# Last attention layer: the zero test of the score sums, one turn of the loop later

## The chip, the cores and the metric

The kernel runs on one core of a Trainium2 chip. The metric is the device time of one execution in microseconds (us); the median of several runs counts. The engines are called by the profile's names: PE (matrix products), DVE (vector), ACT (activations), POOL (GpSimd), SP (issues the DMAs).

## The reference

Four layers run over 64 graphs of 128 nodes with 384 features: an attention over a masked adjacency, two kinds of directed graph convolution (the second kind twice), and a last attention. Ahead of each layer stands a layer norm with ReLU, and its result is added to x. Only the last layer is touched. Per graph it is, cut to what matters (12 heads of 32 features, k = 128 keys):

```
h = maximum(layernorm(x), 0)
q, k, v = heads of h @ Wq.T, h @ Wk.T, h @ Wv.T + bv
a = einsum('bnhd,bmhd->bhnm', q, k) * SCALE + encoding_bias[:, None]
pad_mask = all(a == 0, axis=-1)
a = where(pad_mask[..., None], -inf, a)
a = nan_to_num(softmax(a, axis=-1))
o = einsum('bhnm,bmhd->bnhd', a, v)
x = x + o @ Wo.T + bo
```

A row of scores that is zero throughout gives a row of zeros in a. The kernel does this by a factor per row and head, called keep: 1 if the row's minus-maximum or the sum of its scores is not zero, else 0.

## The kernel before, in words

Each engine has a program of its own for a layer; semaphores tie them. In an attention layer every engine's program is one function, step, that is run for the turns t = 0, 1, 2, ... and writes the order of that engine's work out by hand. A turn works on several graphs at once: a helper called as f(n_, k) works on graph t + k, and n_.has(k) says whether that graph exists. Turns 0 to 3 and the last ones are unrolled, those between are a loop whose body holds two turns. In a turn, graph t gets its scores, t + 1 its projections q and k, t + 2 its norm, t − 1 its probabilities and their product with v, t − 2 its scaling, output projection and result. Tiles that live over a turn have two slots, by t mod 2 (keep and the minus-maxima are among them; the score sums, nonzero, rsum and rnorm have one).

**PE**, in a turn: the scores (L834), then it waits for attended of t − 2 and turns it (L859), projects q and k of t + 1 (lines 149 to 151, weights by hT), projects the output of t − 2 (lines 149 to 151, w by oT), turns the probabilities of t − 1 (L841), projects v (lines 149 to 151), turns h of t + 2 (L804) and multiplies probabilities by v (L850 to L852). Each product is three, as both sides are split into a high and a low half-precision part.

**DVE**, in a turn: row_sums (the reciprocal of the sums that PE's product gave, L697), drop_masked (in the last layer only a wait for the adjacency tile), row_scales (rnorm = rsum × scale × keep, L704), score_bias (L644), attend (attended = product × rnorm, L713), stats (L621), the first four heads of biased_max (scores and their maxima, L665), mean_var, o_split (L718), four heads, var_eps (L630, L631), four heads; score_sums of t − 1 (L673), nonzero_sums (L677), kept_rows (L681), add_result of t − 2 (L725), three p_split (L692), v_split (v_lo, L686), turned_lo (hT_lo, L652).

**POOL**, in a turn: add_out_bias (L499), norm (L483, L485), fold_scores (L505, then L509: the 128 scores of each row and head are added to 64 and to 32 sums; score_sums adds those to one). It waits for all maxima of the turn before it folds.

**ACT**, in a turn: exponentials (L550), o_split (L577), q_evict (L557), normed (L537), k_evict (L562), three p_split (L572), v_split (v_hi, L567), turned_hi (L543).

A helper waits by `wait(dve, semaphore, value)`, an instruction of its own, also for results of its own engine. In the loop the value is a register worked out from the loop's index the first time that a turn of the body needs it. ssum and nonzero are written and read by DVE alone, and in the engine's order; the next writer of ssum waits only for POOL.

```
def nonzero_sums(n_, k):
    wait(dve, ssum_ready, n_.done(k, base=0))
    dve.tensor_scalar(nonzero[:, :], ssum[:, :], 0.0, None, ALU.not_equal).then_inc(nonzero_ready, 1)

def kept_rows(n_, k):
    wait(dve, nonzero_ready, n_.done(k, base=0))
    dve.scalar_tensor_tensor(out=keep[:, n_.slot(k), :], in0=nmax[:, n_.slot(k), :], scalar=0.0,
                             in1=nonzero[:, :], op0=ALU.not_equal, op1=ALU.max).then_inc(keep_ready, 1)
```

Of the kernel before, what the change touches and what calls it, by code (L numbers as in the profile page):

```python
# [139 lines left out]
def wait(eng, sem, value):  # L140

    if isinstance(value, int) and value <= 0:
        return
    eng.wait_ge(sem, value)
# [9 lines left out]
def build(nc, ins, out):  # L154
    with ExitStack() as ctx:
        def sb(stack, name, shape, dt=F32):
            return stack.enter_context(nc.sbuf_tensor(name, shape, dt))
# [189 lines left out]
        def attention(tag, weights, last_layer, next_weights, extras, bias_rows=None, v_bias=None, minus_beta=None, out_bias=None):  # L347
# [7 lines left out]
            with ExitStack() as s:  # L355
# [72 lines left out]
                with nc.Block() as block:  # L428
# [186 lines left out]
                    def _(dve):  # L615
                        dve.wait_ge(tables_ready, 1)

                        def stats(n_, k):
                            if not last_layer:
                                wait_apart(dve, (x_loaded, n_.done(k, 16)))  # L620
                            dve.bn_stats(bn[:, :], x[:, n_.graph(k), :]).then_inc(stats_done, 1)  # L621

                        def mean_var(n_, k):
                            wait_apart(dve, (stats_done, n_.done(k)))
                            dve.bn_aggr(mv[:, :], bn[:, :]).then_inc(mean_ready, 1)

                        def var_eps(n_, k):
                            wait(dve, ln_ready, n_.done(k - 1))
                            wait(dve, mean_ready, n_.done(k))
                            dve.tensor_scalar(ve[:, 0:1], mv[:, 1:2], EPS_PRE, None, ALU.add)  # L630
                            dve.tensor_scalar(ve[:, 1:2], mv[:, 0:1], -1.0, None, ALU.mult).then_inc(var_ready, 1)  # L631

                        def drop_masked(n_, k):
                            wait(dve, adj_loaded, n_.done(k, 16))
                            if not last_layer:
                                wait(dve, bias_ready, n_.done(k - 1))
                                dve.tensor_scalar(drop[:, :], adj_tile[:, n_.slot(k), :], 0.0, -MASKED, ALU.is_le,
                                                  ALU.mult).then_inc(drop_ready, 1)

                        def score_bias(n_, k):  # L640

                            a = adj_tile[:, n_.slot(k), :]
                            if last_layer:
                                dve.tensor_scalar(bias[:, n_.slot(k), :], a, -1.0, None, ALU.mult).then_inc(bias_ready, 1)  # L644
                            else:
                                wait(dve, drop_ready, n_.done(k))
                                dve.scalar_tensor_tensor(out=bias[:, n_.slot(k), :], in0=a, scalar=minus_beta[:, 0:1],
                                                         in1=drop[:, :], op0=ALU.mult, op1=ALU.add).then_inc(bias_ready, 1)

                        def turned_lo(n_, k):  # L650
                            wait(dve, hT_hi, n_.done(k))
                            dve.tensor_tensor(hT[1][:, n_.slot(k), :], hT_bank[:, 0:D], hT[0][:, n_.slot(k), :],  # L652
                                              ALU.subtract).then_inc(hT_lo, 1)
# [21 lines left out]
# [8 lines that stand above are left out]
# [12 lines left out]
                        def row_sums(n_, k):  # L695
                            wait(dve, pv_psum, n_.done(k))
                            dve.reciprocal(rsum[:, :], pv[:, :, HD]).then_inc(rsum_ready, 1)  # L697
# [11 lines left out]
                        def attend(n_, k):  # L709
                            wait(dve, rnorm_ready, n_.done(k))  # L710

                            wait(dve, oT_psum if last_layer else xsum_ready, n_.done(k - 1, base=0))
                            dve.tensor_tensor(attended[:, :].rearrange("p (h e) -> p h e", h=H), pv[:, :, 0:HD],  # L713
                                              rnorm[:, :].unsqueeze(2).to_broadcast([P, H, HD]), ALU.mult).then_inc(attended_ready, 1)
# [13 lines left out]
                        def step(n_):  # L728
                            if isinstance(n_.t, int) and n_.t == 0:
                                for k in (0, 1):  # L730
                                    stats(n_, k)
                                    mean_var(n_, k)
                                    var_eps(n_, k)
                                turned_lo(n_, 0)
                                weights.find_scales(dve)


                                dve.tensor_scalar(q_unscale[:, :], unscale[:, 0:1], -float((D if last_layer else HD) ** -0.5),
                                                  None, ALU.mult).then_inc(setup, 1)
                                turned_lo(n_, 1)  # L740
                                extras["dve_before"](dve)
                                weights.split_low(dve)
                                dve.wait_ge(setup, setups)
                                if "dve_after" in extras:
                                    extras["dve_after"](dve)
                                weights.ready(dve)
                                drop_masked(n_, 0)
                                score_bias(n_, 0)

                            if n_.has(-2):  # L750
                                row_sums(n_, -2)
                            if n_.has(1):
                                drop_masked(n_, 1)
                            if n_.has(-2):
                                row_scales(n_, -2)
                            if n_.has(1):
                                score_bias(n_, 1)
                            if n_.has(-2):
                                attend(n_, -2)
                            if n_.has(2):  # L760
                                stats(n_, 2)
                            if n_.has(0):
                                biased_max(n_, 0)
                            if n_.has(2):
                                mean_var(n_, 2)
                            if last_layer and n_.has(-2):
                                o_split(n_, -2)
                            if n_.has(0):
                                biased_max(n_, 1)
                            if n_.has(2):  # L770
                                var_eps(n_, 2)
                            if n_.has(0):
                                biased_max(n_, 2)
                            if last_layer and n_.has(-1):
                                score_sums(n_, -1)
                            if last_layer and n_.has(-1):
                                nonzero_sums(n_, -1)
                            if last_layer and n_.has(-1):
                                kept_rows(n_, -1)
                            if last_layer and n_.has(-2):  # L780
                                add_result(n_, -2)
                            if n_.has(-1):
                                for c in range(C):
                                    p_split(n_, -1, c)
                            if n_.has(0):
                                v_split(n_, 0)
                            if n_.has(2):
                                turned_lo(n_, 2)
                            if next_weights and isinstance(n_.t, int) and n_.t >= phase.tasks - phase.last:
                                next_weights.largest(dve, 1 if n_.has(0) else 2)  # L790
# [588 lines left out]
        for tag, phase, base, weights, next_weights, kinds in (  # L1379
                ("L1", Phase(0, first=4, last=6, after=2), 0, W1, W2, ("only",)),  # L1380
                ("L2", TwoLayerPhase(G, first=3, last=3, after=2), G, W2, W3, ("first", "second"))):
            with ExitStack() as s:
                w_hi, w_lo = (sb(s, f"{tag}_w_{a}", [P, 3 * len(kinds), C, D], F16) for a in ("hi", "lo"))
                bias_rows = sb(s, f"{tag}_bias_rows", [P, len(kinds), D], F16)
                kept_rows = sb(s, f"{tag}_gain_offset_biases", [P, len(kinds), 4, D])
# [85 lines left out]
```

## Time and profile before

| | |
|---|---|
| median of three runs | 2752.53 us (2752.3 to 2755.15) |
| the profiled execution, its own time | 2754.08 us |
| its span in the profile | 2752.5 us |
| granted clock of PE, mean | 0.979 |
| last attention layer in the span | from about 2050 us to the end |
| busy over the span: PE, DVE, ACT, POOL | 2520.6, 2336.4, 1804.1, 1453.0 us |

Times in the rows are microseconds from the span's start. A timeline row has an instruction's start, its duration, engine, line, operation, what it writes and reads, and how many instructions are merged (x3). The words in brackets at its end say how long the engine sat idle before it and what ended that. Matmuls are pipelined: successive starts tell more of them than durations do.

### The profile page before, as it was taken

What the parts mean: (1) busy time and instruction counts of PE and PEld (TensorE: products, weight loads), DVE (VectorE), ACT (ScalarE), POOL (GpSimd) and SP (SyncE); (2) the same over time, 40 slices, a digit from 0 to 9 for tenths busy, and PEclk for the clock granted to TensorE, in tenths of its full rate; (3) what the DMA queues carried; (4) which work ended last, traced back from release to release, by engine and by line L of the source; (5) the groups of instructions that cost most, each with busy time, mean ns of one, the idle gap of its engine ahead of it and who ended that gap; (6) DMA issues with size and microseconds to landing.
All of it is one profiled execution on the core that took longest, in us unless ns stands there. A gap on an engine that the chain in (4) does not pass through costs nothing. (4 is left out here: it accounts for less than half of the span.)

```text
span 2752.5 us, 86859 instructions
## 1 busy us (share of the span) xinstructions
PE 2520.6 (92%) x27969; PEld 1884.4 (68%) x27969; DVE 2336.4 (85%) x9515; ACT 1804.1 (66%) x4409; POOL 1453.0 (53%) x2016
## 2 busy tenths in 40 slices
PE   5999999986999999699999999999969999999998
PEld 4888888874666665466666666666648888888886
DVE  5778777776999999688888888888859999999997
ACT  5888888874555555455555555555538777777775
POOL 1233232324777777477777777777734434444443
PEclk9999999997999999799999999999979999999998
DMA  3011010102000000100000000000000000000000
GB/s 105 28 30 29 28 30 27 30 14 88 9 9 10 10 10 9 46 10 10 10 10 10 10 10 10 10 10 10 10 6 22 24 25 23 27 23 27 23 27 23
DMA packets 73988, 60.19 MB, mean 22 GB/s; under 512 B 7888, under 2 KB 73936, under 8 KB 73936
## 3 DMA queue, kind: packets, MB, share of 16 engines
q1 hardware_dynamic: 73936, 59.54, 7.1%
q8 instruction: 27, 0.44, 0.1%
q14 instruction: 25, 0.20, 0.0%
HBM read 46.92 MB, written 12.58 MB: 22 GB/s over the span
## 5 line engine op out<-in xcount | busy, mean ns | idle before, releaser
L149 PE MATMUL bank<-L_w_hi,L_hT_hi 128*128 128x384 f16 x2112 | 691.7, 327 | 0.0
L151 PE MATMUL bank<-L_w_hi,L_hT_lo 128*128 128x384 f16 x2112 | 691.5, 327 | 0.0
L150 PE MATMUL bank<-L_w_lo,L_hT_hi 128*128 128x384 f16 x2112 | 691.4, 327 | 0.0
L550 ACT ACTIVATE raw_weights<-L_minus_scores,L_minus_max 128x128 f32<-128x128 f32 x1536 | 476.0, 389 | 69.5 <-DVE L_minus_max L665 67.7
L149 PE MATMUL bank<-L_hT_hi,L_w_hi 128*128 128x128 f16 x2304 | 413.4, 220 | 1.7 <-issue 1.2
L150 PE MATMUL bank<-L_hT_lo,L_w_hi 128*128 128x128 f16 x2304 | 413.3, 220 | 0.0
L151 PE MATMUL bank<-L_hT_hi,L_w_lo 128*128 128x128 f16 x2304 | 413.2, 220 | 0.0
L665 DVE CUSTOM_DVE_ANT_0 L_minus_scores<-bank,L_minus_score_bias 128x128 f32<-128x128 f32 x1536 | 347.8, 282 | 11.4 <-PE bank L834 5.9
L692 DVE TENSOR_TENSOR L_pT_lo<-bank,L_pT_hi 128x512 f16<-128x512 f32 x384 | 241.0, 682 | 126.6 <-ACT L_pT_hi L572 126.5
L1069 ACT ACTIVATE L_e<-bank,L_nmax 128x128 f32<-128x128 f32 x192 | 70.6, 368 | 365.6 <-DVE L_nmax L1154 365.6
L151 PEld LDWEIGHTS bank<-L_w_hi,L_hT_lo 128*128 128x128 f16 x2112 | 207.5, 98 | 138.2 <-issue 2.5
L483 POOL TENSOR_TENSOR L_ln_scale_bias<-L_var_eps,minus_half 128x1 f32<-128x1 f32 x128 | 70.5, 551 | 403.0 <-DVE L_var_eps L631 397.1
L150 PEld LDWEIGHTS bank<-L_w_lo,L_hT_hi 128*128 128x128 f16 x2112 | 207.5, 98 | 108.5 <-issue 2.2
L149 PEld LDWEIGHTS bank<-L_w_hi,L_hT_hi 128*128 128x128 f16 x2112 | 207.9, 98 | 98.7 <-issue 1.7
L491 POOL TENSOR_TENSOR L_xsum<-L_attended,L_bias_v 128x384 f32<-128x384 f32 x64 | 64.1, 1001 | 385.8 <-DVE L_attended L713 385.8
L1014 POOL TENSOR_TENSOR L_right_lo<-L_right,L_right_hi 128x384 f16<-128x384 f32 x192 | 211.3, 1101 | 75.6 <-ACT L_right_hi L1075 74.9
L1003 POOL TENSOR_TENSOR L_cln_scale_bias<-L_cvar_eps,minus_half 128x1 f32<-128x1 f32 x192 | 106.1, 552 | 235.1 <-DVE L_cvar_eps L1222 235.1
L149 PEld LDWEIGHTS bank<-L_hT_hi,L_w_hi 128*128 128x128 f16 x2304 | 227.1, 99 | 2.7 <-issue 2.5
L150 PEld LDWEIGHTS bank<-L_hT_lo,L_w_hi 128*128 128x128 f16 x2304 | 227.1, 99 | 0.7
L572 ACT ACTIVATE L_pT_hi<-bank 128x512 f16<-128x512 f32 x384 | 201.0, 596 | 40.4 <-PE bank L841 40.4
L151 PEld LDWEIGHTS bank<-L_hT_hi,L_w_lo 128*128 128x128 f16 x2304 | 227.1, 99 | 0.0
L1029 POOL TENSOR_TENSOR L_ob<-L_og,L_gain_offset_biases 128x384 f32<-128x384 f32 x192 | 191.4, 997 | 20.1 <-POOL L_og L1019 9.8
(165 smaller groups left out, 7531.3 us busy)
## 6 DMA issues: line engine op xcount, KB each, us to landing
adj_tile<-in_adj SPq DMA_DIRECT2D x320, 64.0 KB, 1.8
x<-in_x SPq DMA_DIRECT2D x64, 192.0 KB, 2.3
out<-L_result SPq DMA_DIRECT2D x64, 192.0 KB, 1.9
raw_weights<-in_L_gnn_Wq SPq DMA_DIRECT2D x2, 576.0 KB, 4.0
raw_weights<-in_L_gnn_Wk SPq DMA_DIRECT2D x2, 576.0 KB, 5.7
raw_weights<-in_L_gnn_Wv SPq DMA_DIRECT2D x2, 576.0 KB, 5.5
raw_weights<-in_L_gnn_Wl SPq DMA_DIRECT2D x2, 576.0 KB, 4.9
raw_weights<-in_L_gnn_Ws SPq DMA_DIRECT2D x2, 576.0 KB, 4.8
```

Of the source, the lines that this page charges most:

```text
L149: pe.matmul(out, stat[0], move[0], start=first, stop=False)
L150: pe.matmul(out, stat[0], move[1], start=False, stop=False)
L151: return pe.matmul(out, stat[1], move[0], start=False, stop=last)
L483: pool.tensor_tensor(ln[:, 0:1], ve[:, 0:1], minus_half[:, :], ALU.pow).then_inc(rstd_ready, 1)
L550: last = act.activation(probs[:, n_.slot(k), i, :], scores[:, i, :], ACT.Exp, bias=nmax[:, n_.slot(k), i:i + 1], scale=-1.0)
L572: act.activation(pT[0][:, HC * c:HC * c + HC, :], pT_banks[c][:, :].rearrange("p (h q) -> p h q", h=HC), ACT.Copy).then_inc(pT_hi[c], 1)
L665: last = dve.tensor_tensor_reduce(scores[:, i, :], s_banks[j][:, c128(c)], bias[:, n_.slot(), :], 1.0, -LOWEST, ALU.add, ALU.min, nmax[:, ...
L692: dve.tensor_tensor(pT[1][:, hs, :], pT_banks[c][:, :].rearrange("p (h q) -> p h q", h=HC), pT[0][:, hs, :], ALU.subtract).then_inc(pT_lo[ ...
L1003: pool.tensor_tensor(cln[:, 0:1], cve[:, 0:1], minus_half[:, :], ALU.pow).then_inc(d["crstd_ready"], 1)
L1014: pool.tensor_tensor(rightv[1][:, :], right[:, :], rightv[0][:, :], ALU.subtract).then_inc(d["r_lo"], 1)
L1029: pool.tensor_tensor(ob[:, :], og[:, :], tables[n_.kind(k)][1], ALU.add).then_inc(d["tail_ready"], 1)
L1069: act.activation(e[:, :], u_bank[:, 0:P], ACT.Exp, bias=nmax[:, 0:1], scale=scalev, accum_out=zsum[:, :]).then_inc(d["p_ready"], 1)
```

## The change

In the last attention layer, nonzero_sums and kept_rows of a graph are done by DVE one turn later: no longer behind score_sums of the same graph, but at the head of the next turn, on both sides of drop_masked, between row_sums and row_scales, which reads keep. The instructions are the same, and each graph still has one of each. score_sums stays where it is.

```diff
@@ -749,8 +749,12 @@
 
                             if n_.has(-2):
                                 row_sums(n_, -2)
+                            if last_layer and n_.has(-2):
+                                nonzero_sums(n_, -2)
                             if n_.has(1):
                                 drop_masked(n_, 1)
+                            if last_layer and n_.has(-2):
+                                kept_rows(n_, -2)
                             if n_.has(-2):
                                 row_scales(n_, -2)
                             if n_.has(1):
@@ -773,10 +777,6 @@
                                 biased_max(n_, 2)
                             if last_layer and n_.has(-1):
                                 score_sums(n_, -1)
-                            if last_layer and n_.has(-1):
-                                nonzero_sums(n_, -1)
-                            if last_layer and n_.has(-1):
-                                kept_rows(n_, -1)
                             if last_layer and n_.has(-2):
                                 add_result(n_, -2)
                             if n_.has(-1):
```

## Rows read from the trace of the kernel before

**Rows 1.** Busy us of each engine (x instructions), granted clock, DMA share; 80 us, last layer.
```profile
2370.00:2450.00 80.00, 74.44 (x1138) 64.22 (x1137) 76.29 (x311) 62.25 (x161) 33.73 (x37) 1.00 0.08 26
```

**Rows 2.** Waits, 2130 to 2690 us: engine line waited for, us in total, times, longest.
```profile
ACT L_v_hi L567 <- PE bank L151: 39.6, 52, 0.8
...
PE bank L859 <- DVE L_attended L713: 36.7, 53, 0.8
...
DVE L_v_lo L686 <- ACT L_v_hi L567: 13.5, 52, 0.3
...
DVE L_rnorm L704 <- DVE L_rsum L697: 5.0, 26, 0.2
```

**Rows 3.** Timeline of all engines, second half of DVE's turn: start us, us, engine, line.
```profile
2399.71 0.55 DVE L673 TENSOR_REDUCE L_score_sum<-L_sums_of 128x12 f32<-128x384 f32 x1
...
2399.89 1.82 POOL L505 TENSOR_TENSOR L_sums_of<-L_minus_scores 128x768 f32<-128x768 f32 x1
...
2400.30 1.45 DVE L677 TENSOR_SCALAR L_nonzero_sum<-L_score_sum 128x12 f32<-128x12 f32 x1
...
2400.98 0.33 PE L151 MATMUL bank<-L_w_hi,L_oT_lo 128*128 128x384 f16 x1
...
2401.77 0.17 DVE L681 SCALAR_TENSOR_TENSOR L_keep<-L_minus_max,L_nonzero_sum 128x12 f32<-128x12 f32 x1
...
2401.78 1.58 ACT L572 ACTIVATE L_pT_hi<-bank 128x512 f16<-128x512 f32 x3 [0.49 <-PE bank L841]
...
2401.95 0.62 DVE L725 SCALAR_TENSOR_TENSOR L_result<-bank,weight_unscale,L_xsum 128x384 f32<-128x384 f32 x1
...
2402.48 1.88 DVE L692 TENSOR_TENSOR L_pT_lo<-bank,L_pT_hi 128x512 f16<-128x512 f32 x3
...
2402.81 1.00 POOL L499 TENSOR_TENSOR L_xsum<-x,L_out_bias 128x384 f32<-128x384 f32 x1
...
2404.12 0.49 ACT L567 ACTIVATE L_v_hi<-bank 128x384 f16<-128x384 f32 x1 [0.76 <-PE bank L151]
```

**Rows 4.** The same timeline from v_lo to PE's turning of attended, and POOL's next.
```profile
2404.64 0.56 DVE L686 TENSOR_TENSOR L_v_lo<-bank,L_v_hi 128x384 f16<-128x384 f32 x1 [0.28 <-ACT L_v_hi L567]
...
2405.11 0.55 DVE L652 TENSOR_TENSOR L_hT_lo<-bank,L_hT_hi 128x384 f16<-128x384 f32 x1
...
2405.58 0.22 DVE L697 RECIPROCAL L_rsum<-bank 128x12 f32<-128x12 f32 x1
...
2405.89 0.23 DVE L704 SCALAR_TENSOR_TENSOR L_rnorm<-L_rsum,weight_unscale,L_keep 128x12 f32<-128x12 f32 x1
...
2406.04 0.22 DVE L644 TENSOR_SCALAR L_minus_score_bias<-adj_tile 128x128 f32<-128x128 f32 x1
...
2406.18 0.55 DVE L713 TENSOR_TENSOR L_attended<-bank,L_rnorm 128x384 f32<-128x384 f32 x1
...
2406.78 0.55 PE L859 MATMUL bank<-identity,L_attended 128*128 128x128 f32 x3 [0.60 <-DVE L_attended L713]
...
2409.60 0.55 POOL L483 TENSOR_TENSOR L_ln_scale_bias<-L_var_eps,minus_half 128x1 f32<-128x1 f32 x1 [5.79 <-DVE L_var_eps L631]
```

**Rows 5.** The same timeline, the next turn, DVE alone.
```profile
2416.07 0.22 DVE L697 RECIPROCAL L_rsum<-bank 128x12 f32<-128x12 f32 x1
...
2416.49 0.23 DVE L704 SCALAR_TENSOR_TENSOR L_rnorm<-L_rsum,weight_unscale,L_keep 128x12 f32<-128x12 f32 x1 [0.19 <-DVE L_rsum L697]
...
2416.84 0.56 DVE L713 TENSOR_TENSOR L_attended<-bank,L_rnorm 128x384 f32<-128x384 f32 x1
```

**Rows 6.** L677's durations (ns min/median/max); its last instance; chain that ended last.
```profile
L677 DVE TENSOR_SCALAR L_nonzero_sum<-L_score_sum x64: 172/1430/1449, 2072.2 to 2736.3; 128x12 f32<-128x12 f32 x64
...
2736.32 0.17 DVE L677 TENSOR_SCALAR L_nonzero_sum<-L_score_sum 128x12 f32<-128x12 f32 x1
...
2736.52 0.17 DVE L681 SCALAR_TENSOR_TENSOR L_keep<-L_minus_max,L_nonzero_sum 128x12 f32<-128x12 f32 x1
...
2728.46 1.43 DVE L_nonzero_sum L677
```

## The prediction

> **What bounds the kernel now.** I read four views: the busy table of a stretch in the middle of the last layer, the list of waits there, the timeline of all engines over one turn of its loop, and the spread of one line's durations.
>
> The busy table shows PE at 74.5 and DVE at 76.3 us of an 80 us stretch, at a granted clock of 1.00, which is the 2.4 GHz level [rows 1]. Two engines that are both nearly full don't tell which sets the pace, so the waits must. In 560 us (53 turns) PE has one wait that returns every turn: the turning of attended (L859) waits for DVE's L713, 36.7 us over 53 times, 0.69 us a turn [rows 2]. DVE has one too, for ACT's v_hi ahead of v_lo (L686), 13.5 us over 52 times, 0.26 us a turn; and ACT ahead of v_hi waits for PE's v projection, 39.6 us over 52 [rows 2]. So the pace is set by a closed ring: PE's projection of v ends, ACT rounds v_hi, DVE makes v_lo and hT_lo, the row sums, the row scales, the bias and attended, PE turns attended and works without another returning wait until the next projection of v ends.
>
> One turn shows it. v_hi starts on ACT at 2404.12 and v_lo on DVE at 2404.64 [rows 3, 4]; then DVE has six instructions back to back, the last, L713, from 2406.18 to 2406.73, and PE goes on with L859 at 2406.78 [rows 4]. The turn after has its row sums 10.49 us later, at 2416.07 [rows 4, 5]; over the 53 turns of those 560 us a turn is 10.57 us, two of them (the loop's body holds two) 21.1.
>
> The reader should see that DVE's turn has two halves. From v_lo to attended each nanosecond is on the ring. From attended to the last p_split it is not, because DVE then sits idle 0.26 us for v_hi [rows 2].
>
> **What the change removes from the second half.** nonzero_sums (L677) is twelve columns wide, and yet it lasts 1.45 us, from 2400.30 to 2401.75; POOL's fold L505 runs from 2399.89 to 2401.71 [rows 3]. Over 64 instances it is 172 ns at the least and 1430 in the middle; the 172 is that at 2736.32, in the last turns, where the code has no graph left to fold [rows 6]. So some 1.26 us of it is a stall behind POOL and 0.17 is work. The Trainium skill (SBUF — State Buffer, "Who interferes with whom") states that a tensor_scalar in a mode that uses both ports and a GpSimd instruction exclude each other for the whole of whichever began first, while tensor_reduce doesn't take part; the trace agrees, since L673 beside it lasts 0.55 under the same fold.
>
> With kept_rows (L681) DVE gets back from 2400.30 to 2401.95, 1.65 us a turn. Where does it go? add_result (L725) is next and needs the output projection, whose last matmul (L151 on oT_lo) starts at 2400.98 and lasts 0.33 [rows 3]. DVE would be there at about 2400.3 and wait till about 2401.35: 1.0 us becomes a new wait on PE. L725 is then done at 1.97 instead of 2.57, and the first p_split (L692) needs ACT's L572, which starts at 2401.78 and does three in 1.58 us: the first is there at about 2402.35, against L692's start at 2402.48 [rows 3]. That is 0.1 us gained, the other two go by ACT's pace and end some 0.2 to 0.3 earlier, and all of it ends in the wait for v_hi, which PE and ACT time. Worth on the ring: 0.
>
> The exception is the end of the layer, where no next projection stands between: there the chain that ended last goes through L677, for 1.43 us, once [rows 6]. What is late behind it there is again ACT's and PE's work, so I take −0.5 us once, between 0 and −1.4.
>
> **What it adds to the first half.** Between L697 (row sums) and L704 (row scales) now stand L677 and L681. Each waits for a result on its own engine, and so does L704. No DMA is moved, and SP's and POOL's orders stay; drop_masked in the last layer is a wait alone, for an adjacency tile loaded a turn ahead.
> - Links without a stall: L677 starts at 2736.32 and L681 at 2736.52, so 0.20 us from start to start; L681 lasts 0.17, and with the same 0.03 its follower comes 0.20 later [rows 6]. L677 itself need not wait for L697: two DVE instructions without a wait stand 0.15 apart (L704 at 2405.89, L644 at 2406.04) [rows 4].
> - New distance from L697 to L704: 0.15 + 0.20 + 0.20 = 0.55 us, or up to 0.05 more for the two further wait instructions: 0.60.
> - Old distance: 0.31 in one turn of the loop (2405.58 to 2405.89) [rows 4], 0.42 in the other (2416.07 to 2416.49) [rows 5]. The 0.11 between the two I read as register work for the semaphore values, which the first of the two turns does anew; the same value is now needed ahead of L677, where it may lie behind L697 or not.
> - Added: 0.24 to 0.29 in the one turn; 0.13 to 0.18 in the other if the register work is hidden, 0.24 to 0.29 if it isn't. L704 to L713 stays as it is.
>
> The wait that L704 had for L697 (5.0 us over 26 times [rows 2]) is already in the old distance. The lower bound is 0.14 us a turn: all hidden work at its best in both turns. The upper bound takes nothing as overlapped: 0.17 + 0.17 for the two, 0.04 twice for the releases and 0.11 of register work, 0.53 us. I take 0.28, near the sum from the rows of this place, since the unrolled rows have constants for waits and the loop's have not.
>
> All of it counts: PE already waits for attended in every turn, so each delay there is a delay of the ring. 64 graphs × 0.28 = 17.9, less 0.5: **+17.4 us**. Bounds: 64 × 0.14 − 0.5 = +8.5, and 64 × 0.53 = +34.
>
> In its new place L677 won't meet POOL: POOL's L499 ends at 2403.81, 1.9 us before, and POOL's next begins at 2409.60 after an idle time of 5.79 [rows 3, 4]. The result is earlier, but L499 stands behind both folds on POOL, so it stays where it is against max.
>
> The profiled execution took 2754.08 us with a span of 2752.5; the median is 2752.53, so span and median may be set equal. Forecast: 2752.5 + 17.4 = 2769.9, say **2770 us**.
>
> **The rivals.**
> 1. Faster: the freed 1.65 us is on the ring after all. This would need DVE's second half to be late for v_lo, that is, the idle time ahead of L686 to be nothing; or p_split to hold PE's product with v, and through it the row sums, by more than hT_lo does. It decides as soon as the second half, not PE, ends last. Then the gain is limited by PE's wait of 0.69 us, as PE is busy for the rest: 64 × 0.69 = 44, so down to 2708 us. For it: DVE's share is the highest of all [rows 1], and the stall is real. Against it: the idle time of 0.26 in 52 of 52 [rows 2]; and the first half only grows. Who counts DVE's busy time alone would forecast the whole stall, 64 × 1.26 = 81 us, but PE's 0.69 a turn caps it. Chance 0.07. (The rule of the Trainium skill named above says that the stall is gone once the two don't overlap, and nothing on who gains by it.)
> 2. No difference: in part of the turns attended isn't what PE waits for, or the two small instructions slip into gaps (L697 to L704 has 0.09 to 0.20 idle already) and the rest is paid back by turns that start earlier. Nearest bound +8.5; to be within 5.5 us it takes less than 0.09 a turn. 2753 to 2758 us. Chance 0.08.
> 3. Much slower: L677 meets POOL in its new place too, now on the ring. It would take POOL's L499 to end 1.9 us later against the row sums. Price 64 × 1.26 = 81 us on top, 2850 us. Chance 0.02.
> 4. The forecast, +8.5 to +34, 2761 to 2786 us: chance 0.83.
>
> **How the numbers follow.** A measurement of this kernel tells about 0.2%, 5.5 us, from no change. Slower by more is cases 3 and 4, 0.85; within is case 2, 0.08; faster is case 1, 0.07. The range is that of case 4, stretched by 1 us at the lower end: 2760 to 2786 us, which leaves out the rest of cases 2, 1 and 3, 0.17 in all.
>
> **What would show it.** In the profile after: L677 at about 172 ns throughout and DVE's busy time down by about 80 us; L697 to L704 at 0.55 to 0.70 us; PE's wait before L859 up from 0.69 to about 0.97 a turn; two turns at about 21.7 us instead of 21.1; a new wait of DVE before L725 for PE's L151, about 1.0 us a turn; POOL's durations as before. I am wrong if two turns take less than 21.1 (then the second half was on the ring), if L677 stays long, or if PE's wait grows and the period doesn't.

## The result and the profile after

The changed kernel takes 2769.69 us (median of four, 2767.88 to 2772.03), the kernel before 2752.44 (median of four). The ratio is 1.0061, with a 95% interval of 1.0043 to 1.0078: **slower by 17 us**, 0.6%. The profiled execution took 2770.96 us with a span of 2769.4, which is 16.9 over the span before.

From the profile's page after: busy time, share of the span and number of instructions for each engine.

```profile
PE 2519.3 (91%) x27969; PEld 1884.5 (68%) x27969; DVE 2254.4 (81%) x9515; ACT 1804.5 (65%) x4409; POOL 1448.0 (52%) x2016
```

DVE is busy for 2254.4 us instead of 2336.4, 82 us less, and the kernel is slower. The list of waits after, 2130 to 2690 us (engine, line, what was waited for, us in total, times, longest), to be read beside [rows 2]:

```profile
DVE L_result L725 <- PE bank L151: 58.0, 51, 1.2
...
PE bank L859 <- DVE L_attended L713: 49.5, 52, 1.0
...
DVE L_pT_lo L692 <- ACT L_pT_hi L572: 18.3, 51, 0.4
...
DVE L_v_lo L686 <- ACT L_v_hi L567: 17.8, 52, 0.3
```

PE's wait for attended went from 36.7 us over 53 times, 0.69 a turn, to 49.5 over 52, 0.95. DVE has a new wait of 58.0 us over 51, 1.14 a turn, for PE's output projection, and a second new one, 0.36 a turn, for ACT's pT_hi. Its wait ahead of v_lo went from 0.26 to 0.34. POOL's L505 lasts 1.82 us as before. Now the timeline of DVE after, with POOL's fold and PE's turning of attended put in (start, duration, engine, line): the end of one turn's first half, then a second turn from score_sums on. It answers [rows 3 to 5].

```profile
2403.93 0.22 DVE L697 RECIPROCAL L_rsum<-bank 128x12 f32<-128x12 f32 x1
...
2404.57 0.23 DVE L704 SCALAR_TENSOR_TENSOR L_rnorm<-L_rsum,weight_unscale,L_keep 128x12 f32<-128x12 f32 x1
...
2404.93 0.56 DVE L713 TENSOR_TENSOR L_attended<-bank,L_rnorm 128x384 f32<-128x384 f32 x1
...
2409.04 0.55 DVE L673 TENSOR_REDUCE L_score_sum<-L_sums_of 128x12 f32<-128x384 f32 x1
...
2409.22 1.82 POOL L505 TENSOR_TENSOR L_sums_of<-L_minus_scores 128x768 f32<-128x768 f32 x1
...
2410.76 0.62 DVE L725 SCALAR_TENSOR_TENSOR L_result<-bank,weight_unscale,L_xsum 128x384 f32<-128x384 f32 x1 [1.17 <-PE bank L151]
...
2411.74 1.89 DVE L692 TENSOR_TENSOR L_pT_lo<-bank,L_pT_hi 128x512 f16<-128x512 f32 x3 [0.36 <-ACT L_pT_hi L572]
...
2413.97 0.56 DVE L686 TENSOR_TENSOR L_v_lo<-bank,L_v_hi 128x384 f16<-128x384 f32 x1 [0.34 <-ACT L_v_hi L567]
...
2414.91 0.22 DVE L697 RECIPROCAL L_rsum<-bank 128x12 f32<-128x12 f32 x1
...
2415.05 0.11 DVE L677 TENSOR_SCALAR L_nonzero_sum<-L_score_sum 128x12 f32<-128x12 f32 x1
...
2415.27 0.17 DVE L681 SCALAR_TENSOR_TENSOR L_keep<-L_minus_max,L_nonzero_sum 128x12 f32<-128x12 f32 x1
...
2415.54 0.23 DVE L704 SCALAR_TENSOR_TENSOR L_rnorm<-L_rsum,weight_unscale,L_keep 128x12 f32<-128x12 f32 x1
...
2415.83 0.55 DVE L713 TENSOR_TENSOR L_attended<-bank,L_rnorm 128x384 f32<-128x384 f32 x1
...
2416.43 0.55 PE L859 MATMUL bank<-identity,L_attended 128*128 128x128 f32 x3 [0.92 <-DVE L_attended L713]
...
2426.73 0.56 DVE L713 TENSOR_TENSOR L_attended<-bank,L_rnorm 128x384 f32<-128x384 f32 x1
```

The row of before that belongs to the last of these:

```profile
2427.41 0.55 DVE L713 TENSOR_TENSOR L_attended<-bank,L_rnorm 128x384 f32<-128x384 f32 x1
```

Four things are to be seen. First, behind L673 DVE has no stall left; it waits 1.17 us for the last matmul of the output projection instead, then for ACT. Second, v_lo still starts out of an idle time, so nothing of what was saved has reached the ring. Third, on the ring the distance from L697 to L713 is 0.92 us in this turn (2414.91 to 2415.83) and 1.00 in the one before (2403.93 to 2404.93), where it was 0.60 and 0.77 [rows 4, 5]. Fourth, two turns, from one start of L713 to the next but one, now take 21.80 us (2404.93 to 2426.73), where they took 21.23 (2406.18 [rows 4] to 2427.41). Over 55 turns in the middle of the layer, which repeat alike, a turn is 10.90 us on average against 10.62: 0.28 more, which is the added distance. The spread of L677 after (ns, min/median/max):

```profile
L677 DVE TENSOR_SCALAR L_nonzero_sum<-L_score_sum x64: 107/109/111, 2077.2 to 2760.2; 128x12 f32<-128x12 f32 x64
```

### The profile page after: what moved, and what is told of

Same layout as the page of the kernel before. It is cut to its first block and busy times, and to the rows that moved or that the text cites. A ratio compares the mean times of both kernels' runs of the same rounds, so it can differ in the third digit from the quotient of the medians.

```text
span 2769.4 us, 86920 instructions
## 1 busy us (share of the span) xinstructions
PE 2519.3 (91%) x27969; PEld 1884.5 (68%) x27969; DVE 2254.4 (81%) x9515; ACT 1804.5 (65%) x4409; POOL 1448.0 (52%) x2016
## 5 line engine op out<-in xcount | busy, mean ns | idle before, releaser
L149 PE MATMUL bank<-L_w_hi,L_hT_hi 128*128 128x384 f16 x2112 | 691.2, 327 | 0.0
L151 PE MATMUL bank<-L_w_hi,L_hT_lo 128*128 128x384 f16 x2112 | 691.1, 327 | 0.0
L149 PE MATMUL bank<-L_hT_hi,L_w_hi 128*128 128x128 f16 x2304 | 414.7, 221 | 1.7 <-issue 1.2
L151 PE MATMUL bank<-L_hT_hi,L_w_lo 128*128 128x128 f16 x2304 | 414.4, 221 | 0.0
L151 PEld LDWEIGHTS bank<-L_w_hi,L_hT_lo 128*128 128x128 f16 x2112 | 207.3, 98 | 137.9 <-issue 2.2
L149 PEld LDWEIGHTS bank<-L_w_hi,L_hT_hi 128*128 128x128 f16 x2112 | 207.8, 98 | 98.5 <-issue 1.5
L149 PEld LDWEIGHTS bank<-L_hT_hi,L_w_hi 128*128 128x128 f16 x2304 | 227.7, 99 | 2.7 <-issue 2.5
L151 PEld LDWEIGHTS bank<-L_hT_hi,L_w_lo 128*128 128x128 f16 x2304 | 227.6, 99 | 0.0
## 6 DMA issues: line engine op xcount, KB each, us to landing
raw_weights<-in_L_gnn_Wq SPq DMA_DIRECT2D x2, 576.0 KB, 4.0
raw_weights<-in_L_gnn_Wk SPq DMA_DIRECT2D x2, 576.0 KB, 5.6
raw_weights<-in_L_gnn_Wv SPq DMA_DIRECT2D x2, 576.0 KB, 5.5
raw_weights<-in_L_gnn_Wl SPq DMA_DIRECT2D x2, 576.0 KB, 5.2
raw_weights<-in_L_gnn_Ws SPq DMA_DIRECT2D x2, 576.0 KB, 4.9
```

The lines of the kernel that those rows point to most:

```text
L149: pe.matmul(out, stat[0], move[0], start=first, stop=False)
L151: return pe.matmul(out, stat[1], move[0], start=False, stop=last)
```

## The experiments

The ratio of each run is to the kernel before, run on the same chip in the same session; the medians of before in those sessions were 2753.0 to 2753.8 us, and the sessions had three different chips, so small differences between two rows of medians say less than the ratios do. "Layer" is the time from the start of the first L713 of the last attention layer to that of the last, in the profiled execution; it leaves out what happens in the other layers. The line numbers of a few kernels are shifted by 1 to 4, since they have lines more (L677 is L680 in the padded ones, L859 is L862 or L861).

| kernel | median us | ratio to before, 95% interval | layer us | against 666.9 |
|---|---|---|---|---|
| before | 2752.44 | | 666.9 | |
| changed | 2769.69 | 1.0061 (1.0043 to 1.0078) | 682.8 | +15.9 |
| e1_gap | 2753.15 | 0.9999 (0.9989 to 1.0009) | 666.8 | −0.1 |
| e2_kept_only | 2755.07 | 1.0006 (0.9996 to 1.0016) | 668.9 | +2.0 |
| e3_nonzero_first | 2764.73 | 1.0041 (1.0026 to 1.0056) | 678.9 | +12.0 |
| e4_after_pad | 2769.20 | 1.0053 (1.0035 to 1.0071) | 682.8 | +15.9 |
| e5_before_pad | 2756.99 | 1.0013 (1.0003 to 1.0022) | 670.3 | +3.4 |
| e6_bias_behind | 2760.47 | 1.0029 (1.0018 to 1.0041) | 666.5 | −0.4 |
| e7_short_ring | 2751.80 | 0.9997 (0.9987 to 1.0006) | 657.9 | −9.0 |
| e8_stats_on_ring | 2776.88 | 1.0093 (1.0076 to 1.0110) | 691.9 | +25.0 |
| e9_short_ring_last | 2743.69 | 0.9967 (0.9955 to 0.9979) | 657.9 | −9.0 |
| e10_after_pad5 | 2785.61 | 1.0116 (1.0100 to 1.0131) | 698.0 | +31.1 |
| e11_bias_first_layer | 2761.31 | 1.0028 (1.0018 to 1.0038) | 667.0 | +0.1 |

The diffs below are cut: conditions such as `if last_layer and n_.has(-1)` are left out where they aren't the point.

The theory under test: a turn of the last layer is a ring, PE's projection of v, v_hi, v_lo to attended on DVE, PE; what DVE does between attended and v_lo has slack, and what it does between v_lo and attended counts one to one. The rival is that DVE's total work, with the stall in it, matters.

### The saving alone (e1_gap)

```diff
 score_sums(n_, -1)
-nonzero_sums(n_, -1)
-kept_rows(n_, -1)
 add_result(n_, -2)
 for c in range(C): p_split(n_, -1, c)
+nonzero_sums(n_, -1)
+kept_rows(n_, -1)
 v_split(n_, 0)
```

> The kernel before with nonzero_sums and kept_rows of t - 1 moved behind the three p_split, ahead of v_split, in the same turn: DVE's idle time for v_hi, where POOL's folds and L499 are just over. This frees the second half of DVE's turn of the stall and puts nothing into the first. Ring theory (the pace is PE, v_hi, v_lo to attended): L677 at 0.11 to 0.17 us, DVE busy 80 us less, time as before, 2752 us within 3. Rival (the stall of 1.26 us was holding the turn): 10 to 44 us less than before.

Measured: no difference, 0.9999, with DVE busy for 2258.1 us, 78 less than before. Timeline of DVE in e1_gap:

```profile
2403.72 0.16 DVE L677 TENSOR_SCALAR L_nonzero_sum<-L_score_sum 128x12 f32<-128x12 f32 x1
...
2403.92 0.17 DVE L681 SCALAR_TENSOR_TENSOR L_keep<-L_minus_max,L_nonzero_sum 128x12 f32<-128x12 f32 x1
...
2404.15 0.56 DVE L686 TENSOR_TENSOR L_v_lo<-bank,L_v_hi 128x384 f16<-128x384 f32 x1
```

L677 lasts 0.16 us here and in nearly all of its 64 instances, so the stall is gone. One instance lasts 0.78 us, at the end of the layer (2730.88), where POOL's second fold, L509, still runs. v_lo starts 0.06 us behind the end of kept_rows. Waits of the same kernel:

```profile
DVE L_result L725 <- PE bank L151: 60.3, 53, 1.2
...
PE bank L859 <- DVE L_attended L713: 36.7, 53, 0.8
```

PE's wait for attended is 36.7 us over 53 times, to the digit that of [rows 2]. So 78 us of DVE's time were worth nothing that the time shows: the rival that forecast a gain falls, and the slowdown comes from the new place at the head.

### Work put into the slack, and too much of it (e4_after_pad, e10_after_pad5)

```diff
 def score_sums(n_, k):
     wait(dve, quarter_ready, n_.done(k, base=0))
+    for spare in spares:
+        dve.tensor_reduce(spare[:, :], quarter[:, :, :], AX.X, ALU.add)
     dve.tensor_reduce(ssum[:, :], quarter[:, :, :], AX.X, ALU.add).then_inc(ssum_ready, 1)
```

on the changed kernel, with two spare tiles (e4) or five (e10).

> The changed kernel with two more tensor_reduce like score_sums, into spare tiles, in the second half of DVE's turn: about 0.95 us of work more a turn, 61 us in all. DVE has about 1.1 us of wait before L725 there. Ring theory: the wait before L725 shrinks by 0.95 us and the time stays, 2769 us within 3. Rival (DVE's total work sets the pace): up to 61 us more, 2830 us.

> The changed kernel with five spare reductions (0.47 us each from start to start, 2.35 us a turn) in the second half instead of the two of e4_after_pad, which left the time alone. The waits of the second half in the changed kernel sum to 1.1 (for L151) + 0.36 (for pT_hi) + 0.34 (for v_hi) = 1.8 us. Ring theory: once these are used up the second half takes the pace, 0.4 to 0.6 us a turn over, 25 to 38 us more than the changed kernel, about 2800 us. Rival (DVE has still other slack, or none of it counts): as the changed kernel.

Two: no difference from the changed kernel (2769.20 against 2769.69; the layer is 682.8 us in both). Waits of e4_after_pad:

```profile
PE bank L862 <- DVE L_attended L716: 50.3, 52, 1.0
...
DVE L_result L728 <- PE bank L151: 11.1, 51, 0.3
```

The wait for PE's L151 has shrunk from 1.14 us a turn to 0.22, and PE's own is as in the changed kernel: the pad was taken out of the slack. Five: 16 us over the changed kernel, less than the 25 to 38 expected. DVE in e10_after_pad5, one turn:

```profile
2413.80 2.38 DVE L675 TENSOR_REDUCE L_spare<-L_sums_of 128x12 f32<-128x384 f32 x5
...
2416.10 0.54 DVE L676 TENSOR_REDUCE L_score_sum<-L_sums_of 128x12 f32<-128x384 f32 x1
...
2416.56 0.61 DVE L728 SCALAR_TENSOR_TENSOR L_result<-bank,weight_unscale,L_xsum 128x384 f32<-128x384 f32 x1
...
2418.88 0.54 DVE L689 TENSOR_TENSOR L_v_lo<-bank,L_v_hi 128x384 f16<-128x384 f32 x1
```

No idle time of DVE is left in the turn; the second half now ends last. The miss is in how I had sized the slack. An idle time is counted from an instruction's end, but without a wait between them two instructions overlap: score_sums (L676) lasts 0.54 us and L728 starts 0.46 after it. Three waits that go return 0.08 to 0.09 us each on top of their 1.8, so the slack was about 2.1 us, and five pads take 2.30 (2413.80 to 2416.10, where score_sums starts). The turns agree: in the middle of the layer one takes 11.08 us against 10.90 in the changed kernel, 0.18 more, which puts the slack at 2.12. Over these 55 turns that is 9.8 us of the 15.2 by which the layer is longer; 4.8 more came in the last five turns, for which no cause is shown, and 0.6 in the first three.

### Is L677 slow, or does it wait for POOL? (e5_before_pad)

The same two pads on the kernel before.

> The kernel before with the same two spare reductions ahead of the stalled L677. If L677's 1.43 us is a wait for POOL's fold to end, L677 still ends with it and so shrinks by what was put ahead, to about 0.5 us, and the time stays, 2752 us within 3. Rival (L677 is slow by itself in this place): it stays at 1.43 us, the second half grows by 0.95 us against an idle time of 0.26, and the kernel takes about 64 x 0.7 = 45 us more.

Measured: 1.0013, 3 to 4 us more. POOL's fold and DVE's L677 (here L680), and the row scales of two later turns:

```profile
2412.30 1.82 POOL L506 TENSOR_TENSOR L_sums_of<-L_minus_scores 128x768 f32<-128x768 f32 x1
...
2413.64 0.51 DVE L680 TENSOR_SCALAR L_nonzero_sum<-L_score_sum 128x12 f32<-128x12 f32 x1
...
2418.35 0.23 DVE L707 SCALAR_TENSOR_TENSOR L_rnorm<-L_rsum,weight_unscale,L_keep 128x12 f32<-128x12 f32 x1 [0.19 <-DVE L_rsum L700]
...
2429.11 0.23 DVE L707 SCALAR_TENSOR_TENSOR L_rnorm<-L_rsum,weight_unscale,L_keep 128x12 f32<-128x12 f32 x1 [0.20 <-issue]
```

L680 begins 0.92 us later against the end of the maxima than it did (1.50 us behind it instead of 0.58), and lasts 0.51 instead of 1.43: the fold ends at 2414.12 and it ends at 2414.15. It is a wait for POOL's instruction to end, and the pads fitted into it. The Trainium skill (SBUF — State Buffer, "Who interferes with whom") has it that the one that began first keeps the ports for its whole instruction; the trace agrees. The 3 us have another place: ahead of row scales there is now an idle time of 0.19 to 0.20 us in both turns of the loop's body, where before only one of them had it [rows 4, 5]. 0.10 × 32 turns is 3.2 us. Why the second turn has it here isn't shown: its instructions and waits on DVE are in the same order as before, and the list of waits puts this idle time (5.3 us over 27 times) down to no other engine. That stays open.

### The two halves of the price (e2_kept_only, e3_nonzero_first)

e2 moves kept_rows alone; e3 is the changed kernel with one more swap.

```diff
 row_sums(n_, -2)
 drop_masked(n_, 1)
+kept_rows(n_, -2)
 row_scales(n_, -2)
 ...
 nonzero_sums(n_, -1)
-kept_rows(n_, -1)
```

```diff
+nonzero_sums(n_, -2)
 row_sums(n_, -2)
-nonzero_sums(n_, -2)
 drop_masked(n_, 1)
 kept_rows(n_, -2)
 row_scales(n_, -2)
```

> The kernel before with kept_rows alone moved to the head of the next turn, behind drop_masked; nonzero_sums keeps its old place and its stall. kept_rows then waits for nothing new: it stands 0.14 behind L697, and L704 comes 0.27 after it (the changed kernel's distance), so L697 to L704 is 0.42 in both kinds of turn, against 0.31 and 0.42 before. Ring theory: 0 to 0.11 us a turn, 0 to 7 us more than before, about 2756 us, of the 17 of the whole change; nonzero_sums is then the larger part. Rival (kept_rows' wait on DVE's own result at the head is the price): most of the 17 us, 2766 us or more.

> The changed kernel with nonzero_sums ahead of row_sums instead of behind. Its link to kept_rows then runs beside L697: from the first of the four instructions to L713 it should take about 0.78 us in the one turn and 0.85 in the other, where the changed kernel has 0.92 and 1.00. Ring theory: 64 x 0.14 = 9 us less than the changed kernel, about 2761 us, 8 us over before. Rival (the price is that keep is late as such, or not these links): as the changed kernel, 2769 us.

e2 costs 2.0 us of layer. Its time is not told apart from that of before (1.0006, interval 0.9996 to 1.0016). The rows of two turns:

```profile
2407.30 0.22 DVE L697 RECIPROCAL L_rsum<-bank 128x12 f32<-128x12 f32 x1
...
2407.44 0.11 DVE L681 SCALAR_TENSOR_TENSOR L_keep<-L_minus_max,L_nonzero_sum 128x12 f32<-128x12 f32 x1
...
2407.65 0.23 DVE L704 SCALAR_TENSOR_TENSOR L_rnorm<-L_rsum,weight_unscale,L_keep 128x12 f32<-128x12 f32 x1
...
2417.84 0.22 DVE L697 RECIPROCAL L_rsum<-bank 128x12 f32<-128x12 f32 x1
...
2418.30 0.23 DVE L704 SCALAR_TENSOR_TENSOR L_rnorm<-L_rsum,weight_unscale,L_keep 128x12 f32<-128x12 f32 x1
```

L697 to L704 is 0.35 and 0.46 us against 0.31 and 0.42 before: 0.04 a turn, × 64 = 2.6 us. I had expected 0.42 in both. kept_rows hides beside L697 as long as it waits for nothing, and the register work of the one turn stays. So of the 0.275 us a turn that the whole change costs, 0.04 is kept_rows by itself, and the rest is nonzero_sums and the wait of kept_rows for it.

e3 is 5 us faster than the changed kernel (9 expected), by the layer 3.9; in the middle of the layer a turn is 0.085 us shorter, 5.4 over 63. The layer shows less because one of the last turns took 10.19 us against 8.87; the granted clock was 0.83 there against 1.00 (from 2734.5 to 2744.7 us and, in the changed kernel, from 2742.1 to 2751.0). Its rows:

```profile
2409.96 0.16 DVE L677 TENSOR_SCALAR L_nonzero_sum<-L_score_sum 128x12 f32<-128x12 f32 x1
...
2410.03 0.23 DVE L697 RECIPROCAL L_rsum<-bank 128x12 f32<-128x12 f32 x1
...
2410.23 0.17 DVE L681 SCALAR_TENSOR_TENSOR L_keep<-L_minus_max,L_nonzero_sum 128x12 f32<-128x12 f32 x1
...
2410.79 0.55 DVE L713 TENSOR_TENSOR L_attended<-bank,L_rnorm 128x384 f32<-128x384 f32 x1
```

From the first of the four to L713 it is 0.83 us, where the changed kernel has 0.92: 0.09 × 64 = 5.8 us. The overlap works as thought, but L677 lasts 0.16 us here against 0.11 behind L697, and L681 follows 0.27 after it instead of 0.22. That is the part of the 9 us that didn't come.

### One to one? (e8_stats_on_ring)

```diff
+if last_layer and n_.has(2): stats(n_, 2)
 attend(n_, -2)
-if n_.has(2): stats(n_, 2)
+if not last_layer and n_.has(2): stats(n_, 2)
```

> The kernel before, where stats (L621, 0.47 us from start to start) stands ahead of attend instead of behind it. No engine has more or less work. Ring theory, one to one: 60 turns x 0.47 = 28 us more, less what the wait for rnorm hides (0 to 0.1 a turn), 2775 to 2781 us. Rival (there is some slack between attended and PE): clearly less than 20 us more.

```profile
2414.49 0.23 DVE L704 SCALAR_TENSOR_TENSOR L_rnorm<-L_rsum,weight_unscale,L_keep 128x12 f32<-128x12 f32 x1
...
2414.77 0.55 DVE L621 BATCH_NORM_STATS2 L_bn<-x 128x6 f32 x1
...
2415.24 0.54 DVE L713 TENSOR_TENSOR L_attended<-bank,L_rnorm 128x384 f32<-128x384 f32 x1
```

L704 to L713 is 0.75 us, where it was 0.29 and 0.35 [rows 4, 5]: 0.46 and 0.40 added, 0.43 on average, × 60 = 26 us. The layer is 25.0 longer and the kernel 23 us slower. One instruction with no effect on any engine's total, moved from the slack onto the ring, costs its whole distance. It is slightly under the 28 of the plain product because in one kind of turn only 0.40 of its 0.47 us is added: L713 stood there 0.35 us behind L704 and not 0.29, and part of that time is now covered.

### Shortening the ring (e6, e7, e9, e11)

e6 is e1_gap with score_bias behind attend; e7 puts turned_lo there too; e9 is e7 in the last layer alone; e11 is the kernel before with score_bias behind attend in the first attention layer alone. The diff is that of e7 against e1_gap:

```diff
 row_scales(n_, -2)
-score_bias(n_, 1)
 attend(n_, -2)
+if last_layer and n_.has(1) and not (isinstance(n_.t, int) and n_.t == 0):
+    turned_lo(n_, 1)
+score_bias(n_, 1)
 ...
-if n_.has(2): turned_lo(n_, 2)
+if not last_layer and n_.has(2): turned_lo(n_, 2)
```

> e1_gap with score_bias (L644, 0.15 us from start to start) moved from ahead of attend to behind it. L713 waits for rnorm anyway (0.26 us from L704 to L713 in the unrolled turns without L644), so only 0.03 to 0.09 us a turn leave the ring: 2 to 6 us less than before, about 2750 us. Rival (each instruction ahead of attend counts in full): 9 us less.

> e6_bias_behind with turned_lo (L652, 0.47 us on the ring) moved behind attend, so a turn later than it was. The product that row_sums needs is ready about 0.2 us before L697 now starts, so L697 can come 0.2 to 0.25 earlier, no more; and PE needs hT_lo right behind its turning of attended, where it will wait 0.1 to 0.2. Ring theory: 0.05 to 0.3 us a turn less, 3 to 18 us under before, about 2743 us. Rival (another thing than DVE's first half, such as PE alone, sets the turn): as before or slower through PE's new wait, 2752 to 2765 us.

> e7_short_ring with both moves (turned_lo and score_bias behind attend) in the last attention layer only; the first attention layer is again as before. In e7_short_ring the first layer's row sums spread over 583.8 us instead of 576.1, while its last layer went from 666.9 to 657.9 us between the first L713 and the last. Ring theory: the loss of the first layer was score_bias's move there, and 9 us less than before remain, about 2744 us. Rival (what e7_short_ring gained was made up by chance elsewhere): 2752 us.

> The kernel before with score_bias moved from ahead of attend to behind it in the first attention layer only. If that is what cost e6_bias_behind its time, 7 to 8 us more than before, about 2760 us; if the cost was in the last layer, as before, 2752 us.

e6 went the wrong way, 7 us slower than before. The table shows that the last layer isn't at fault (−0.4 us). The edit stood in code that both attention layers share. Row sums of the first attention layer (line, durations in ns, first and last start), in the kernel before, in e6 and in e11:

```profile
L697 DVE RECIPROCAL L_rsum<-bank x64: 220/222/232, 52.9 to 628.9; 128x12 f32<-128x12 f32 x64
```

```profile
L697 DVE RECIPROCAL L_rsum<-bank x64: 223/223/233, 53.3 to 637.0; 128x12 f32<-128x12 f32 x64
```

```profile
L697 DVE RECIPROCAL L_rsum<-bank x64: 219/220/233, 53.1 to 636.7; 128x12 f32<-128x12 f32 x64
```

They spread over 576.0 us before, 583.7 in e6 and 583.6 in e11. e11 as a whole is 8 us slower, which accounts for e6. Why the first layer loses by this move is not shown. In the last layer, taking L644 from between L704 and L713 gained nothing against e1_gap, because L713 waits for rnorm nearly as long: it starts 0.27 and 0.35 us behind L704, where it was 0.28 and 0.35.

e7 was as before in sum, with 9.0 us gained in the last layer and 7.7 lost in the first. e9 keeps the gain alone: **2743.69 us, 0.9967 (0.9955 to 0.9979) of the kernel before**, faster than both kernels. Its ring and its waits:

```profile
2408.93 0.56 DVE L686 TENSOR_TENSOR L_v_lo<-bank,L_v_hi 128x384 f16<-128x384 f32 x1
...
2409.63 0.23 DVE L697 RECIPROCAL L_rsum<-bank 128x12 f32<-128x12 f32 x1
...
2410.41 0.56 DVE L713 TENSOR_TENSOR L_attended<-bank,L_rnorm 128x384 f32<-128x384 f32 x1
```

```profile
DVE L_result L725 <- PE bank L151: 34.3, 54, 0.7
...
PE bank L863 <- DVE L_attended L713: 24.9, 53, 0.6
...
PEld bank L149 <- issue: 5.7, 26, 0.2
```

v_lo is followed by the row sums 0.70 us later instead of 0.94 (0.47 twice), with an idle time of 0.14 us in between: they now wait for PE's product, whose last matmul starts at 2409.41 and lasts 0.18. PE's wait for attended is down from 0.69 to 0.47 us a turn, and DVE still has 0.64 us of wait before L725. A ring that is 0.24 us shorter would give 15 us; the turns gave 7.5. Of the 9.0 that the layer is shorter, the other 1.5 came in the last five turns: the stall that is gone there (0.5, as in e1_gap) and a last turn at a higher granted clock (0.9, see below). In the loop one kind of turn went from 10.57 to 10.36 us, the other only from 10.67 to 10.62. In this second kind stands a new idle time, 5.7 us over 26 times, 0.22 each, of PE's weight loads (PEld) ahead of L149, behind the turning of attended. In size it is what is missing. The profile names no releaser for it ("issue"). hT_lo, which PE needs for the loads right behind, ends 0.12 us before (L652 from 2400.26 to 2400.81, the load at 2400.93), so a wait for it is likely, but it was not tried by itself.

## Why the prediction was right, step by step

The forecast was 2770 us and the result 2769.7; the sum was +17.4 and the spans differ by 16.9. The mechanism and the main term were right. That the total agrees to 0.5 us is in part luck, since not every term was right by itself.

- **What bounds the kernel.** Right. e1_gap and e4_after_pad show the slack of the second half, e8_stats_on_ring the one-to-one price of the first, e10_after_pad5 the point at which it turns over.
- **The stall.** Right: 1.43 us was POOL's fold (e5_before_pad). L677 fell to 0.11 us rather than the 0.17 expected. Why it is shorter right behind L697 isn't shown; that it waits for nothing can't be the reason alone, since it lasts 0.16 in e3_nonzero_first, where it waits for nothing either. The extra 0.06 is off the busy time and not off the ring: kept_rows still starts 0.22 us behind it. It never met POOL in the new place, its longest instance there being 0.11.
- **The new wait before L725.** 1.0 us expected, 1.14 measured. L725 starts 0.12 us behind the end of PE's last matmul (2410.31 to 2410.64 in the turn above), where the working allowed 0.04, and the idle time is counted from the end of L673, 0.04 before the start that the working took.
- **The added distance.** 0.28 us a turn taken; measured 0.92 − 0.60 = 0.32 in the one turn and 1.00 − 0.77 = 0.23 in the other, 0.275 on average. Inside it two things cancelled. The distance from L697 to L704 was to be 0.55 to 0.60 and is 0.63 and 0.64: the link from L681 to L704 takes 0.27 us (2415.27 to 2415.54), and not the 0.20 that was carried over from another pair, L677 to L681 [rows 6]. And the register work of the one turn, 0.11, which I left open, does get hidden behind L697: both turns now have the same distance. The reading holds in the trace: before, a register instruction (ALU_OP, L64, at 2416.40 for 0.04 us) stands between the wait for rsum and L704 in the turn with 0.42; after, two such instructions of that turn, at 2403.91 and 2404.02, lie ahead of L677, beside L697.
- **The length of a turn.** Two turns were said to go from 21.1 to about 21.7 us, and went from 21.23 to 21.80. The 21.1 came from dividing 560 us by 53 waits; the starts of L713 are exact. The step between them, 0.57, is two times 0.28.
- **The bounds.** The 0.04 us for a release in the upper bound has no row; the nearest is the 0.03 from the end of L677 to L681 [rows 6]. The forecast itself doesn't use it.
- **The end of the layer.** −0.5 us taken; it was about −1.8. From the row sums of the third graph from the end to those of the second it takes 8.87 us (2741.28 to 2750.15) against 9.53 (2723.48 to 2733.01) before, 0.66 less although 0.31 was added: the stall was on the path there for 0.97, about twice the term. And in the last gap PE's turning of the probabilities ran at a different clock. Before, then after:

```profile
2738.74 2.77 PE L841 MATMUL bank<-identity,raw_weights 128*128 128x128 f32 x12
```

```profile
2756.17 1.61 PE L841 MATMUL bank<-identity,raw_weights 128*128 128x128 f32 x12
```

  Twelve transposes took 2.77 us before and 1.61 after. The granted clock was 0.69 in 2733 to 2744 us before and 0.83 in 2750 to 2760 after, both a mix of the 1.2 and the 2.4 GHz level, at a stage where PE waits for DVE and ACT in both kernels. From row sums to row sums it is 9.86 us after against 10.41 before. That this 0.55 (0.86 with the 0.31 added) is the clock's doing was not tried, but the runs bear it out. Between the last two starts of L713 the granted clock was 0.67 in before, e1, e5, e6, e8 and e11, and all six took 10.41 to 10.43 us; it was 0.82 or 0.83 in the changed kernel, e2, e3, e4, e7 and e9, and these took 9.55 to 9.87. (e10, with its pads in that stretch, had 0.68 and 10.75.) So about 0.9 us of the term came from the clock, which the prediction didn't consider.
- **The balance.** 63 turns × 0.275 = 17.3, less 1.8, is 15.5; the layer shows +15.9. The rest of the 16.9 is a first L713 that stands at 2078.0 instead of 2077.1: 0.3 us of this is the distance added to the first graph, which the 63 turns leave out, and 0.6 stands already in the L697 before it (2077.09 against 2076.46), where nothing of the change has run. Here is the luck: the end of the layer gave 1.3 us more than was taken, and this late start gave 0.6 of it back.

## What to carry to other kernels

An engine's busy share says nothing of what an instruction on it is worth. Look for an idle time that returns in every turn: it splits that engine's turn into a half where time is free and a half where it is not, and an operation moved into the second pays its whole distance (0.43 us for one statistic, 25 us in all). The way back can bring less, as something else may become the next limit: a ring 0.24 us shorter gave 0.13 us a turn. A stall in the free half is no reason to act, even one of some 80 us; if it is to be moved, move it within that half, as e1_gap does, and spend the effort on the other half. When an edit stands in a function that several layers share, read the time layer by layer, or restrict it: moving score_bias changed nothing in one attention layer and cost 8 us in the other.

## What the runs showed of the hardware

- A link between two twelve-column DVE instructions where the second waits for the first has no single price: from start to start 0.20 us (L677 to L681 in the unrolled turns before), 0.22 (the same pair after, in the loop) and 0.15 (after, in the unrolled turns at 2741.42 and 2750.29), 0.27 and 0.28 (L681 to L704 after), 0.21 (that pair in a turn of e2_kept_only).
- The same twelve-column L677 lasts 0.11 us right behind L697 (after), 0.16 behind L652 (e3) and behind p_split (e1_gap), 0.17 behind L673, whose result it reads (the last turn of before), and 1.43 when it begins under POOL's fold.
- Idle times of an engine understate its slack. In e10 each wait that goes gives back 0.08 to 0.09 us more than its idle time, because neighbours without a wait overlap.
- Register work for semaphore values lengthened a gap by 0.11 us where it stood behind a wait for the engine's own result, and no longer did where an instruction in flight covered it (0.42 and 0.31 us before, 0.64 and 0.63 after). Not every such gap is register work: in e5 the other turn went from 0.31 to 0.42 too, with no register instruction there.
